# Eight experts for every row, or two: routing the FFN rows of a graph attention kernel through DRAM

## The reference

```
h = einsum('ni,hid->nhd', layernorm(x), W)
e = leaky(a_src[src] + a_dst[dst]); alpha = softmax of e over the edges of one dst
x = x + (sum over edges of alpha * h[src]) @ W_out
t = layernorm(x)
p = softmax(t @ router_w.T); (rw, re) = top_k(p, 2); rw = rw / rw.sum()
combine[row, re] = rw                      # zero for the other six experts
for e in range(8):
    t_out += combine[:, e] * (gelu(t @ w1[e] + b1[e]) @ w2[e] + b2[e])
x = x + t + t_out
```

## Time and profile before

| | |
|---|---|
| runs | 3, from 1541.4 to 2022.45 us |
| median | 1542.62 us |
| span of the profiled execution, first to last instruction | 1540.1 us |
| busy share of the span | PE 91%, PE weight loads 74%, DVE 71%, ACT 64%, POOL 54% |

### The profile page before, as it was taken

How to read it: one execution, slowest core, us unless ns; L and a number is a source line. 1 busy time by engine, 2 the same in 40 slices (tenths; PEclk the granted TensorE clock), 3 DMA queues, 4 the chain that set the end, 5 groups by cost and what they waited for, 6 DMA issues and landing times.

```text
span 1540.1 us, 29587 instructions
## 1 busy us (share of the span) xinstructions
PE 1407.5 (91%) x7327; PEld 1141.6 (74%) x7327; DVE 1098.5 (71%) x3031; ACT 980.3 (64%) x2505; POOL 835.1 (54%) x886
## 2 busy tenths in 40 slices
PE   5925775999999999999999999999999999999998
PEld 4813454788888888888888887878787878787887
DVE  6726765677777777777777787877777777777543
ACT  3714554576767676766667676767676767676732
POOL 1347777665666666565656565656565656561000
PEclk9966867799999999999999999999999999999999
DMA  9564654434343434343434343434434343473000
GB/s 221 145 193 121 193 146 118 128 99 124 107 126 105 125 104 125 104 120 111 117 112 118 114 117 113 117 111 115 114 106 124 102 129 99 133 90 59 1 17 18
DMA packets 89788, 174.83 MB, mean 114 GB/s; under 512 B 22455, under 2 KB 56049, under 8 KB 89593
## 3 DMA queue, kind: packets, MB, share of 16 engines
q0 software_dynamic: 40448, 111.89, 28.1%
q1 hardware_dynamic: 48071, 60.77, 13.2%
q10 hardware_dynamic: 1106, 0.27, 0.1%
HBM read 159.24 MB, written 14.43 MB: 113 GB/s over the span
## 4 chain that ended last, share of the span: by engine, by line
PE 74%; issue 6%; DVE 5%; POOL 4%; ACT 4%; ACTq 1%; DMA 1%; DVEq 0%; POOLq 0%
PE agg_ps L1117 24%; PE ob L1192 20%; PE hb L1146 15%; POOL ring L740 4%; PE kbank L1079 3%; PE ob L1223 2%; PE ob L1146 2%; PE ob L1258 2%; PE ob L1198 1%; ACT acc L1336 1%; DVE ring L848 1%; PE kbank L1095 1%; ACT agg_ps L1339 1%; PE kbank L1094 1%; DVE oh L785 1%
## 5 line engine op out<-in xcount | busy, mean ns | idle before, releaser
L740 POOL DMA_INDIRECT ring<-table,srcE x832 | 803.0, 965 | 504.3 <-PE agg_ps L1117 264.8
L1117 PE MATMUL agg_ps<-ring,oh 128*128 128x260 f32 x1664 | 550.9, 424 | 19.8 <-ACT agg_ps L1339 10.3
L1336 ACT COPY acc<-agg_ps x831 | 307.7, 370 | 188.1 <-PE agg_ps L1117 120.4
L1192 PE MATMUL ob<-w_sb,hT 128*125 128x256 f32 x1600 | 408.4, 380 | 1.6
L1339 ACT COPY agg_ps<-zc 128x260 f32 x832 | 314.6, 378 | 98.6 <-ACT acc L1336 3.2
L1117 PEld LDWEIGHTS agg_ps<-ring,oh 128*128 128x128 f32 x1664 | 292.2, 199 | 86.7 <-issue 55.2
L1192 PEld LDWEIGHTS ob<-w_sb,hT 128*125 128x125 f32 x1600 | 295.8, 188 | 52.7 <-issue 9.6
L848 DVE TENSOR_TENSOR ring<-ring,kbank 128x1024 f32<-128x1024 f32 x208 | 244.7, 1213 | 50.3 <-ACT ring L1358 50.1
L1368 ACT ACTIVATE hT<-hb,b_sb 128x375 f32<-128x375 f32 (+1 forms) x272 | 154.0, 566 | 146.0 <-PE hb L1146 145.1
L983 DVE SCALAR_TENSOR_TENSOR y<-ob,cmb,y 125x256 f32<-125x256 f32 x400 | 188.9, 475 | 46.7 <-PE ob L1192 43.1
L1146 PE MATMUL hb<-xTh,w1l 128*128 128x376 f32 (+1 forms) x544 | 186.3, 423 | 0.0
(11 more groups left out here) (271 smaller groups left out, 1376.8 us busy)
## 6 DMA issues: line engine op xcount, KB each, us to landing
OT<-relb_d SPq DMA_DIRECT2D x52, 512.0 KB
ring<-table,srcE POOLq DMA_INDIRECT x832
y<-in_x_dram SPq DMA_DIRECT2D x50, 125.0 KB
out_dram<-y SPq DMA_DIRECT2D x50, 125.0 KB
table<-hrow SPq DMA_DIRECT2D x25, 227.5 KB
acc<-in_x_dram SPq DMA_DIRECT2D x2, 1568.0 KB
acc<-in_L_ffn_w_dram SPq DMA_DIRECT2D x1, 2048.0 KB, 14.3
w_sb<-in_L_ffn_w_dram SPq DMA_DIRECT2D x1, 2048.0 KB
```

The source lines that it names most:

```text
L740: pool.indirect_dma_start(out=rings[b % RING][:, k, :], out_offset=None, in_=table[:, :], in_offset=bass.IndirectOffsetOnAxis(ap=srcE[:, t ...
L1117: T.matmul(aggf[:, bass.ds(bank_of[k // 8][k % 8], ROW)], oh[:, (4 * b + q) % OHQ, k % 4, :], rings[b % RING][:, k, :], start=False, stop= ...
L1192: t = T.matmul(o[0:Q, 0:D], hT[:, e % 2, f, cols], w2_sb[:, e, f, :], start=f == 0, stop=f == KC - 1)
L1336: A.copy(accf[:, bass.ds(row_of[h][k % 8], ROW)], aggf[:, bass.ds(closed[h][k % 8], ROW)]).then_inc(S["ev"], 1)
```

## The change

Each row goes to its two experts only.

- **Places.** After `best_two`, one-hot masks of both choices are multiplied by a strict upper triangle on PE (bf16), which counts the earlier rows of the same expert. With running totals in `carry` this gives every row two places in a DRAM buffer that has a region for each expert (`positions`).
- **Scatter.** POOL writes each block of normed rows to DRAM twice by indirect DMA (`scatter`: 100 in all, at step 43 of the group).
- **Closings.** The groups form four sets (5, 5, 4 and 3 groups; 15, 15, 12 and 8 blocks). At the end of a set DVE makes a table of row tiles (`tiles_table`): 128 rows of one expert each, 37, 37, 31 and 23 tiles, 128 in all whatever the counts are. SP fills the end of each expert's region with zeros (`fill_ends`: eight DMAs of 128 KB).
- **Tiles.** For each tile SP loads 128 rows (128 KB) and the w1 and b1 of its expert (257 KB, from a copy in DRAM laid out for it, two buffers). PE turns the rows (2), multiplies by w1 (4 fp32 products of 128 columns), ACT applies gelu (2), PE multiplies by w2 in SBUF (2 products of 256 columns) and DVE adds b2. SP stores the tile. The tiles of the first three sets are spread over the slots up to the next closing (310 to 543, 550 to 742, 748 to 887). Those of the last stand one per slot in 892 to 914.
- **Results.** When all tiles of a set are stored, POOL gathers for each block the rows of both experts (100 indirect DMAs), and DVE adds them to `acc` with the row's weights (`final`, two steps). For the first two sets a block takes three slots (551 to 593 and 750 to 792), for the last two one slot (894 to 905 and 921 to 928), with two buffers.
- Gone are the fp32r split, `hidden`, `output`, `accumulate` and the bias products as they were. The router's product is plain fp32.

The core of the diff:

```diff
-                        exact(hbank[f][:, 0:w], [(w1h[:, e, k, fs], w1l[:, e, k, fs]) for k in range(KC)],
-                              [(xTh[:, u, k, 0:w], xTl[:, u, k, 0:w]) for k in range(KC)]).then_inc(S["h1"], 1)
...
+                    def scatter(g):
+                        u = g % 2
+                        pool.wait_ge(S["px"], g + 1)
+                        for i in range(size(g)):
+                            for k in range(2):
+                                pool.indirect_dma_start(out=xr_d[:, :], out_offset=bass.IndirectOffsetOnAxis(ap=idx[0:Q, block_at(g) + i, k:k + 1], axis=0),
+                                                        in_=xn[0:Q, u, i, :], in_offset=None).then_inc(xs_st[u], 16)
+                    def results(b):
+                        s = sg_of[b // GB]
+                        if b == block_at(SGS[s][0]):
+                            for r in range(RY):
+                                pool.wait_ge(yr_st[r], 16 * len(range(r, first_tile[s + 1], RY)))
+                        if b >= RR:
+                            pool.wait_ge(S["cb"], b - RR + 1)
+                        for k in range(2):
+                            pool.indirect_dma_start(out=res[0:Q, b % RR, k, :], out_offset=None, in_=yr_d[s][:, :], ...
...
+                    def load_tile(n):
+                        s, i = sg_tile[n]
+                        r = n % RL
+                        if i == 0:
+                            fill_ends(s)
+                            for g in SGS[s][-2:]:
+                                sp.wait_ge(xs_st[g % 2], scattered(g))
+                            sp.wait_ge(z_st[s], 16 * (NE + 1))
+                        off = loads(ENG.SP, tileI[0:1, s, 0, i:i + 1], BASE[NSG] - P, WHY2)[0]
+                        if n >= RL:
+                            sp.wait_ge(S["xt"], n - RL + 1)
+                        sp.dma_start(rows[:, r, :], xr_d[bass.ds(off, P), :]).then_inc(row_ld[r], 16)
+                    def load_w1(n):
+                        expert = loads(ENG.SP, tileI[0:1, s, 1, i:i + 1], (NE - 1) * P, WHY2)[0]
+                        if n >= RW:
+                            sp.wait_ge(S["gl"], 2 * (n - RW + 1))
+                        sp.dma_start(w1s[:, n % RW, :], w1_d[bass.ds(expert, P), :]).then_inc(w1_ld[n % RW], 16)
+                    def store_tile(n):
+                        sp.wait_ge(S["ye"], n + 1)
+                        sp.dma_start(yr_d[s][i * P:(i + 1) * P, :], ysb[:, n % RY, :]).then_inc(yr_st[n % RY], 16)
...
+                        for sl in range(it * BT, it * BT + BT):
+                            if sl - 5 in tile_at:
+                                store_tile(tile_at[sl - 5])
+                            for n in load_at.get(sl, []):
+                                load_tile(n)
+                            for n in w1_at.get(sl, []):
+                                load_w1(n)
+                            for b in out_at.get(sl, []):
+                                store_block(b)
...
+                    def hidden(n):
+                        pe.wait_ge(w1_ld[n % RW], 16 * (n // RW + 1))
+                        pe.wait_ge(S["xc"], n + 1)
+                        for f in range(KC):
+                            for k in range(KC):
+                                t = T.matmul(hbank[:, f * P:(f + 1) * P], w1s[:, n % RW, k * D + f * P:k * D + (f + 1) * P],
+                                             xTt[:, n % RX, k * P:(k + 1) * P], start=k == 0, stop=k == KC - 1)
...
+                        if sl in tile_at:
+                            turn_rows(tile_at[sl])
+                        if sl - 2 in tile_at:
+                            second_addresses(tile_at[sl - 2])
+                            hidden(tile_at[sl - 2])
+                        if sl - 4 in tile_at:
+                            output(tile_at[sl - 4])
```

More of the change, by code:

```diff
@@ L635, in gnn_ffn_kernel @@
             pr = s2("pr4", [P, GB, 2])
[L636 to L638 removed]
+            wt = s2("wt", [P, NB, 2])
+            RL, RW, RX, RH, RY, RR = 6, 4, 2, 3, 3, 2
+            upper = s2("upper", [P, P], BF16)
+            ones = s2("ones", [P, P], BF16)
+            regions = s2("regions", [P, NSG, NE])
+            one1, one2, at1, at2 = (s2(n, [P, GB, NE]) for n in ("one1", "one2", "at1", "at2"))
@@ L651, in gnn_ffn_kernel @@
+            w1_ld = [sem(f"w1_ld{r}") for r in range(RW)]
+            yr_st = [sem(f"yr_st{r}") for r in range(RY)]
+            res_ld = [sem(f"res_ld{r}") for r in range(RR)]
+            o_st = sem("o_st")
+            z_st = [sem(f"z_st{s}") for s in range(NSG + 1)]
             WHY = "worked out on the chip from a block number that is at most NB - 1"
-            def loads(eng, ap, top_):
+            WHY2 = "worked out on the chip from counts of rows, and within the regions by their sizes"
@@ L708, in _, with store_block @@
+                    def store_block(b):
+                        row = loads(ENG.SP, rotI[0:1, b // GB, b % GB:b % GB + 1], (NB - 1) * Q)[0]
+                        sp.wait_ge(S["cb"], b + 1)
+                        sp.dma_start(out[bass.ds(row, Q), :], acc[0:Q, b, 0:D]).then_inc(o_st, 16)
                     fetch(0)
@@ new lines, in _ @@
+                        p, s0 = place(it)
+                        if p is not None and s0 == 0 and p + 1 < GROUPS:
+                            load_x(p + 1)
+                        for sl in range(it * BT, it * BT + BT):
[7 more added lines that the diff above has]
+                                store_block(b)
@@ L748, in deviations @@
                         gp.tensor_tensor(rstd[0:Q, 0:n], mv[0:Q, 0:n, 1], root_[0:Q, 0:1].to_broadcast([Q, n]), ALU.pow).then_inc(S["sq"], 1)
-                    for it in range(-RING, LAST):
-                        for q in range(QUADS):
-                            p, s0 = place(it)
-                            if p is not None and p + 1 < GROUPS and s0 == BT and q == (3 if behind(p + 1) else 1):
-                                deviations(p + 1)
-                            if it + RING < NBAT:
-                                gathers(it + RING, q)
+                    def scatter(g):
[5 more added lines that the diff above has]
+                                                        in_=xn[0:Q, u, i, :], in_offset=None).then_inc(xs_st[u], 16)
@@ new lines, in _ @@
+                    dev_at = {at(g, 20): g for g in range(GROUPS)}
+                    scatter_at = {at(g, 43): g for g in range(GROUPS)}
+                    for b in range(RING - 1):
+                        for q in range(QUADS):
+                            gathers(b, q)
+                    for sl in range(-BT, LAST * BT):
+                        if sl in dev_at:
+                            deviations(dev_at[sl])
+                        if sl in scatter_at:
+                            scatter(scatter_at[sl])
+                        for b in result_at.get(sl, []):
+                            results(b)
+                        if sl % 4 == 3 and sl // BT + RING < NBAT:
+                            gathers(sl // BT + RING, sl % BT // 4)
@@ L1279, in _ @@
-                    FIRST = (0, 16, 25, 32)
-                    def products(p, s):
-                        if p is not None and 0 <= p < GROUPS:
-                            experts(p, s)
+                        elif s == 39:
+                            pe.wait_ge(S["init"], 5 + NSG)
+                            pe.wait_ge(S["lgc"], g + 1)
+                            pe.wait_ge(S["mm"], g + 1)
+                            n = size(g)
+                            for i in range(n):
+                                o = ob[0:Q, i * NE:(i + 1) * NE]
+                                T.matmul(o, upper[0:Q, 0:Q], both[0:Q, i, :], start=True, stop=i == 0)
+                                for j in range(i):
+                                    T.matmul(o, ones[0:Q, 0:Q], both[0:Q, j, :], start=False, stop=j == i - 1)
+                            for j in range(n):
+                                t = T.matmul(ob[0:Q, 32:32 + NE], ones[0:Q, 0:Q], both[0:Q, j, :], start=j == 0, stop=j == n - 1)
+                            t.then_inc(S["ps"], 1)
```

572 lines of the change are left out of this document (293 added, 279 removed).

## The result

The changed kernel takes 1714.8 us (median of 4 runs, 1711.3 to 1721.3) where the kernel before took 1542.0 beside it: ratio 1.113, 95% interval 1.110 to 1.116. (One of the four runs of the kernel before took 2022 us in a slow state; ratios are formed without such runs.) Forecast were 1600 and 1518 to 1680. The sign was right, the size 172 us instead of 58. The span of the profiled execution is 1709.4 us. Its page, to be read against the earlier trace rows: every engine is less busy in share, and the clock has left its plateau of nines.

What follows compares the result with a forecast made beforehand. The prediction took PE to bound all but the first stages before, and POOL to set the pace after the change. Slot 832 at 1417 us plus a 184 us tail gave 1601, forecast as 1600 us (+3.7%), range 1518 to 1680.

Steps and rivals of the forecast that it cites:

- The first stages: Slots without results: POOL's own program needs 1.43 us per slot and sets the pace.
- The full tail: Behind slot 832: 184 us against 76; group 16 30, closing 20, 23 tiles 99, last tile 6, last blocks 29.
- the signs of being wrong: Edge stage ending before 1370 or after 1470 us, scatters much above 1 us on POOL, tail tiles every 2.5 us.
- The main rival on the other side: Whole kernel: added transfers cost POOL 0.95 us without the gap, tail short; end at 1466 to 1510 us; chance 0.10.
- slot 832 at 1417 us: End of the edge stage, where only the tail is left: 1417 us (1380 to 1460), 47 earlier than before.
- The nearest row is the gather, 128 rows per instruction at 1.25 us: POOL's added scatters and result gathers: 1.25 us each, floor 0.95, upper end 1.6.
- 3% of 1231, 37 us: Edge stage, on top of POOL's 1231 us of work: 37 us for closings, store waits and imperfect filling.
- 59 us for the slots behind the last gather: From slot 783 to slot 832: another 42 to 49 slots at 1.35 us, 59 us.
- POOL as the bound of the whole edge stage: Up to slot 783, POOL's 970 instructions at 1.25 us plus 18 take 1231 us, ending at 1321 instead of 1391.
- The clock rival: PE swings between clocks, mean 0.75: slot 1.55 us, tail tile 5 us, slot 832 at 1470, end 1670; chance 0.23.
- the PE rival: Tail bound by PE, w1 loads hidden: 2.3 us per tile, tail 127 us, end 1507 to 1525; chance 0.17.
- Which fits into 4.3: Tail: twelve result blocks of the third set, 2.5 us each on POOL plus round trip, hidden beside 4.3 us tiles.

Runs made afterwards that it cites:

- g1: Changed kernel with scatters and result gathers of 128 rows instead of 125: 1671.5 us, ratio 1.083 to the kernel before.
- g4: Changed kernel with one result gather per block instead of two (second expert's share missing): 1665.2 us, ratio 1.078 to the kernel before.
- k4: Two w1 buffers instead of four, in the changed kernel with 128-row transfers: ratio 1.191 to the kernel before, against 1.186 with four, second kind of chip.
- e1: Changed kernel with only the result gathers at 128 rows instead of 125: ratio 1.179 to the kernel before, against 1.176 unmodified, second kind of chip.

## Why the prediction was off, step by step

**Confirmed.** The first stages: 1.47 us per slot up to the first closing, forecast 1.43. The full tail, 190 us against 184, and its parts: 39 for 30, 26 for 20, 84 for 99, 41 for 35. PE's share of 60 to 70% (71), the stretches of 2.1 us per slot with results (2.10 and 2.20), where POOL is full. Of the signs of being wrong three came: the edge stage ended after 1470 us (1519), a scatter took much more than 1 us (1.2), and the last tiles followed each other at less than 2.5 us (2.3). The last gather stood at 1442 us and not near 1350, and PE didn't wait for w1 in each tile. The main rival on the other side, cheaper transfers with a short tail, was wrong in both halves.

**The sum that failed is slot 832 at 1417 us: it came at 1519.** The step that failed is the cost of the edge stage: POOL's added transfers, the waits on top, and the rate of the other engines in slots with tiles were all put too low. The 102 us, term by term, as an account of POOL's time up to its last gather and of the slots behind it:

1. "The nearest row is the gather, 128 rows per instruction at 1.25 us", for the scatters and result gathers. They took 1205 and 1227 ns and the gap, 1.51 and 1.53: 84 x 0.26 + 54 x 0.28 = 37 us. 1.53 lies inside the 0.95 to 1.6 that I named, but I carried 1.25 into the sum and no share of the upper end into the range of slot 832. g1 takes out 32 us of this term, and the last gather came 19 us earlier; the whole kernel took 43 us less.
2. 832 gathers at 0.966 and 0.303 instead of 0.95 and 0.30, and the `deviations` about as forecast: 15 us. A mean of many rows (the earlier trace rows had 965) and not two rows of a timeline should have been taken.
3. "3% of 1231, 37 us" for closings, waits at results and imperfect filling: 68 measured, 31 more. I had listed the right places (`fill_ends`, the last store of a set) and priced none of them. The first closing alone is 9.9 us, the first results 9.5, the second results 7.3.
4. 59 us for the slots behind the last gather, at 1.35 us each: they took 77, 18 more. When the last gather was issued 787 tiles had been aggregated, so 45 were left, 1.72 us each. No gather is left for POOL there, so this is what PE, DVE and ACT need for a slot in that stretch, at a granted clock of 0.87 and with a tile every 4.6 slots. My 1.3 to 1.45 for these engines left the clock out.

37 + 15 + 31 + 18 = 101 of 102. The account is complete for POOL, but it isn't a list of causes: where POOL waits for the others, a cheaper transfer only makes it wait longer.

**POOL as the bound of the whole edge stage** is the part of the mechanism that failed. Its own account fills 95% of the stage, but the other 5% lie where they tell: it is full up to slot 287 and in the two stretches with results, and from 336 to 528 and 596 to 720 it fills 96 and 90%, waits for the aggregation, and the slot takes 1.56 and 1.73 us where POOL's own program needs 1.49 and 1.56. g4 took 41 us from it and got 16 back, g1 32 for 19, most of it where POOL is full. The forecast had DVE and ACT at 1.3 to 1.45 us per slot and PE at 1.15, hidden behind POOL's 1.43. The waits in it were those of the attention chain in the kernel before; it had no term for waits inside a tile, nor for a lower clock. How much of the difference is the clock isn't settled for this chip. The clock rival (a chance of 0.23, 1670 us) named something real: PE was granted 1.00 before and 0.83 now, and the products of the aggregation, the same in both kernels, took 490 ns on average instead of 424. From 300 us to the last gather 1335 of them kept PE busy for 505 us, where 1340 had taken 427. These products alone, before and after (PE, PEld, then the last columns of the earlier trace rows):

```profile
300.00:1391.00 1091.00, 427.10 (x1340) 221.92 (x1340) 1.00 0.41 114
300.00:1442.00 1142.00, 504.58 (x1335) 265.86 (x1333) 0.83 0.58 164
```

The mechanism of that rival, PE full at a swinging clock, didn't come: PE was busy 75% of this stretch.

**The tail came out right from wrong parts,** by luck: one is 15 us too long, the other three 9, 6 and 6 too short. The tiles were counted with a loop that the kernel, with four buffers, doesn't have, at 4.3 us; they take 3.7 on average, because results hold DVE and with it the bias sums, and 2.3 at the end, which is the figure of the PE rival (2.3). k4 prices the misread loop at 3.1 per tile. The last loop takes longer than its 29 us, since the landing takes 4.2 to 4.8 us and not 3.2, and the issues 1.53 and not 1.25. "Which fits into 4.3", of the third set's results beside the tiles, was the wrong cover: they were what held the tiles.

## What to carry to other kernels

Before work is taken from the full engine, ask what the next one needs per slot with every new instruction at its own price, the gap behind it too: here 200 more transfers made the engine that had been 60% busy the bound in parts of the edge stage, and 128 rows in place of 125 would have made each a fifth cheaper. Then ask, stretch by stretch, whether that engine really has no wait: a share of 95% over the stage hid that it was the bound in only some of them. Fewer and smaller products also cost the clock: the products that stayed became dearer, 490 ns instead of 424. And work that can only start when all rows are known (closings, a last set, results behind the last store) is paid in full behind the end, 114 us here; it wants a last set as small as possible.

## What the runs showed of the hardware

- An indirect transfer of 125 rows costs POOL 1205 (scatter) and 1227 ns (gather), one of 128 rows of the same 1 KB 996 and 966. The software queue's packets say why it may be: 40448 before the change, 66048 after it and 50048 in g1, so (66048 - 40448) / 200 = 128 packets for a transfer of 125 rows and 48 for one of 128. e1, with half of them at 128 rows, has 58048, just between. The landing in the last loop went from 4.2 to 4.8 us to 2.7 to 3.2.

```profile
q0 software_dynamic: 50048, 138.12, 30.7%
```

  The Trainium skill, "DMA: Bandwidth & Descriptors", section "Why a DMA increments its semaphore by 16 and not by 1", says that a transfer is spread over the largest number of engines up to 16 that divides its rows, by which it would be 16 for 128 and 5 for 125. The longer landing agrees; no run here shows the engines themselves, and the price on POOL isn't on that page.
- The granted clock fell with the products: a mean of 0.955 before and 0.818 after, and on the second kind of chip 0.77, 0.745 and 0.69 to 0.70 with double w1 products, all products and half of a tile's. In the tail of the changed kernel the same eight products took 2.05 us in its first three tiles and 1.13 in its last five. The Trainium skill, "TensorE: Matmul & The Clock Gate", section "HAM oscillation", describes waits between bursts as the cause of such swings, and the rows of the tail agree: from 1560 to 1580 us PE was busy 47% at a granted clock of 0.61, just behind a stretch at 71% and 1.00.
- The same two programs stand 11.3% apart on one kind of chip and 17.6% on the other. A ratio measured on one of them doesn't carry over.
